# Other stage orders in a two-layer transformer kernel: constant stores on a second queue, two gate products ahead of the downs, and rearranged middle and attention stages

## The reference

```python
xn = _layernorm(x)
x = x + TTT(xn) + FFN(xn)          # layer 0
xn = _layernorm(x)
x = x + MLA(xn) + MoE(xn)          # layer 1
```

## Time and profile before

| | |
|---|---|
| median of 3 runs | 2130.93 us (2130.27 to 2133.2) |
| profiled execution | 2132.01 us |
| its span, first to last instruction | 2130.1 us |
| mean granted TensorE clock | 0.966 of full |
| TensorE busy | 1906.4 us, 89% |
| VectorE, ScalarE, GpSimd busy | 57%, 47%, 47% |
| DMA | 297.97 MB, mean 140 GB/s |

### The profile page before, as it was taken

The page is one execution under the profiler, slowest core; times in us unless marked ns, Lnnn a source line. Parts: engine busy times, 40 slices in busy tenths (PEclk is TensorE's granted clock), DMA queues, the critical chain, the costliest instruction groups (busy, mean ns, idle before and its releaser), DMA issues. The chain is left out here.

```text
span 2130.1 us, 34654 instructions
## 1 busy us (share of the span) xinstructions
PE 1906.4 (89%) x12632; PEld 1437.8 (67%) x12632; DVE 1208.6 (57%) x2367; ACT 1009.4 (47%) x2173; POOL 998.5 (47%) x765
## 2 busy tenths in 40 slices
PE   5897988899999999678999789999999999999997
PEld 3675767666666655567777567777777777777775
DVE  4662655686877764355243356555566555655552
ACT  3332646565565655466433235444444444444441
POOL 5443656455655544200233236555555555555551
PEclk9998999999999999789999889999999999999998
DMA  7875647336335432402677751222322223222211
GB/s 256 284 274 195 199 148 249 105 105 210 120 109 174 136 112 82 148 1 94 223 262 248 253 185 41 90 109 89 102 106 110 89 100 109 109 80 90 99 41 59
DMA packets 157111, 297.97 MB, mean 140 GB/s; under 512 B 20240, under 2 KB 97296, under 8 KB 150288
## 3 DMA queue, kind: packets, MB, share of 16 engines
q1 hardware_dynamic: 156944, 295.75, 41.2%
HBM read 221.52 MB, written 74.19 MB: 139 GB/s over the span
## 5 line engine op out<-in xcount | busy, mean ns | idle before, releaser
L1915 POOL TENSOR_SCALAR probs<-probs,rsum 128x512 f32<-128x512 f32 x256 | 397.5, 1569 | 362.1 <-DVE rsum L2047 362.1
L2011 ACT ACTIVATE p_tok<-bank 128x512 fp32r<-128x512 f32 x256 | 154.5, 606 | 403.4 <-PE bank L1955 403.3
L2043 DVE TENSOR_REDUCE nmax<-bank 128x1 f32<-128x512 f32 x256 | 158.9, 683 | 111.5 <-PE bank L1947 111.5
L2053 DVE TENSOR_TENSOR p_tok<-bank,p_tok 128x512 fp32r<-128x512 f32 x256 | 173.8, 681 | 22.6 <-ACT p_tok L2011 22.6
L2003 ACT ACTIVATE probs<-bank,nmax 128x512 f32<-128x512 f32 x256 | 172.2, 694 | 4.2 <-DVE nmax L2043 4.2
L60 PE MATMUL bank<-xs,ffn_w 128*128 128x512 f32 x352 | 153.4, 436 | 10.4 <-issue 8.4
L1955 PE MATMUL bank<-ident,probs 128*128 128x128 f32 x1024 | 156.6, 276 | 6.1 <-DVE p_tok L2053 5.9
L1423 POOL TENSOR_TENSOR y_pieces<-y_tok,y_pieces 128x512 fp32r<-128x512 f32 x48 | 61.6, 1298 | 208.4 <-ACT y_pieces L1635 208.4
L1955 PEld LDWEIGHTS bank<-ident,probs 128*128 128x128 f32 x1024 | 121.8, 141 | 55.3 <-issue 28.3
L1077 DVE SCALAR_TENSOR_TENSOR pt<-bank,t_mask 128x256 f32<-128x256 f32 x256 | 91.7, 414 | 101.1 <-PE bank L864 99.7
L61 PE MATMUL bank<-xs,ffn_w 128*128 128x512 f32 x352 | 138.9, 395 | 0.0
(11 more groups left out here) (271 smaller groups left out, 4906.9 us busy)
## 6 DMA issues: line engine op xcount, KB each, us to landing
ffn_w<-ffn_pieces SPq DMA_DIRECT2D x120, 512.0 KB, 3.6
uvo<-uvo_pieces SPq DMA_DIRECT2D x16, 2048.0 KB, 7.9
wq<-wq_pieces SPq DMA_DIRECT2D x16, 1536.0 KB, 6.4
ffn_pieces<-stage SPq DMA_DIRECT2D x30, 512.0 KB, 4.2
xs<-xn_pieces SPq DMA_DIRECT2D x4, 2048.0 KB, 8.4
y_tok<-in_gup SPq DMA_DIRECT2D x32, 256.0 KB, 3.1
wk<-wk_pieces SPq DMA_DIRECT2D x16, 512.0 KB, 3.6
ffn_w<-ffn_pieces SPq DMA_DIRECT2D x16, 384.0 KB, 3.5
```

The lines of the kernel that those rows point to most:

```text
L1915: nc.gpsimd.tensor_scalar(probs[:, u % 8, :], probs[:, u % 8, :], rsum[:, u % 8:u % 8 + 1], None, ALU.mult).then_inc(norm_done, 1)
L2011: nc.scalar.activation(p_tok[:, Q % 2, 0, :, hh * P:(hh + 1) * P], banks[4 + u % 2][:].rearrange("p (k q) -> p k q", k=NBLK), ACT.Copy).th ...
L2043: nc.vector.tensor_reduce(nmax[:, u % 8:u % 8 + 1], banks[u % HG][:], axis=X_AXIS, op=ALU.max, negate=True).then_inc(max_done, 1)
L2053: nc.vector.tensor_tensor(p_tok[:, Q % 2, 1, :, q], banks[4 + u % 2][:].rearrange("p (k q) -> p k q", k=NBLK), p_tok[:, Q % 2, 0, :, q].bi ...
```

## The change

Eight edits, all of order or of place; no product is added or left out.

1. Stage 1: the constants of the last tile are stored by ScalarE's queue instead of SyncE's, and SyncE issues `move_rates` behind the last tile's work instead of within it.
2. Stage 2's FFN order: two gate products instead of one stand ahead of each part's down products, and ahead of the first part. `wx` is cleared by VectorE, and GpSimd spreads the first keys ahead of its other two clearings.
3. Middle, first steps: the first four transpositions to tokens are issued at once; the bias products are made in four parts in steps -4 to -1; `ow_hi` is scaled by GpSimd, `ow_lo` is made in two halves; normalizing and splitting move by a step.
4. Middle, steps after: `high` and `low` of the older block come ahead of the newer block's normalizing and squaring.
5. Last expert: the eight pieces of the last group are placed as with the other experts (`fills`), and `TAIL` is reordered by one place.
6. Attention's first steps: four key projections in step -1, two in step 0, one each in steps 1 and 2. In the other groups the output products stand ahead of the projections of their slot, and the fourth step has its two query projections in slots 0 and 1 and the context in slot 2.
7. `rope_low` is done ahead of GpSimd's four scalings, and `rope_high` between the second and the third exponential.
8. End: the last group's output weights have a place of their own (`uvo_end`), the output products of the last two groups follow `CLOSING`, and three steps fewer follow at the end.

The diff, cut to these parts:

```diff
         def ffn_order():
-            order = [("gate", 0, 0)]
+            order = [("gate", 0, 0), ("gate", 0, 1)]
             for a, (lo, hi) in enumerate(THIRDS):
                 for i in range(lo, hi):
-                    order += [("gate", a, i)] if i > lo else []
+                    order += [("gate", a, i)] if i > lo + 1 else []
                     order += [("up", a, i)]
-                order += [("gate", a + 1, hi)] if a + 1 < len(THIRDS) else []
+                order += [("gate", a + 1, hi), ("gate", a + 1, hi + 1)] if a + 1 < len(THIRDS) else []
                 order += [("down", a, o) for o in range(NF)]
             return order
...
                                 load_x(t + 2)
-                            if slot == 0 and t == NTB - 1:
-                                move_rates()
-                        store_cst(t)
+                        if t < NTB - 1:
+                            store_cst(t)
+                    move_rates()
...
+                    for m in range(NF):
+                        q = NF * (NTB - 1) + m
+                        act.wait_ge(cst_done, q + 1)
+                        for e in range(2):
+                            act.dma_start(cst_dram[8 * m:8 * m + 8, NTB - 1, e, :, :],
+                                          cs[:, q % NCS, e * HX:(e + 1) * HX]).then_inc(cst_out[q % NCS], 16)
...
-                    nc.gpsimd.memset(wx[:], 0.0).then_inc(zero_done, 1)
+                    spread_k(0)
                     nc.gpsimd.memset(sg_bd[:], 0.0).then_inc(zero_done, 1)
                     nc.gpsimd.memset(grad_bd[:], 0.0).then_inc(zero_done, 1)
-                    spread_k(0)
                     spread_k(1)
...
+                    nc.vector.memset(wx[:], 0.0).then_inc(wx_zero, 1)
...
         uvo, tok = place("uvo", [P, 2, HG, HID], F32R, 24), place("ckv_tok", [P, 2, 2, NBLK, KVC], F32R, 40)
+        uvo_end = place("uvo_end", [P, 2, HG, HID], F32R, 64)
...
-        LAST = NBLK * (NG - 1) + 8
+        LAST = NBLK * (NG - 1) + 5
+
+        CLOSING = {NQD - 3: ((1, NG - 2, 0), (3, NG - 2, 1)), NQD - 2: ((2, NG - 2, 2),),
+                   NQD: ((0, NG - 2, 3), (1, NG - 1, 0), (2, NG - 1, 1)), NQD + 1: ((0, NG - 1, 2), (1, NG - 1, 3))}
 
         def att_jobs(n):
             p, G = (n + 1) % 4, (n + 1) // 4
             slots = [[], [], [], []]
+            if n < 3:
+                early = {-1: (0, 1, 2, 3), 0: (4, 5), 1: (6,), 2: (7,)}[n]
+                slots[0] += [("ctx", n - 1, 0)] if n >= 1 else []
+                for x, j in enumerate(early):
+                    slots[1 + x // 2].append(("proj", 1, j))
+                return slots
+            if p == 3 and G + 1 < NG:
+                return [[("proj", G + 1, 6)], [("proj", G + 1, 7)], [("ctx", n - 1, 0)], []]
             if 1 <= n <= NQD:
                 slots[0].append(("ctx", n - 1, 0))
+            if n >= 7 and p < 2 and (n - 7) // 4 < NG - 2:
+                slots[1].append(("out", (n - 7) // 4, 2 * p))
+                slots[3].append(("out", (n - 7) // 4, 2 * p + 1))
             if G + 1 < NG:
                 slots[1].append(("proj", G + 1, 2 * p))
                 slots[2].append(("proj", G + 1, 2 * p + 1))
-            if n >= 7 and p < 2 and (n - 7) // 4 < NG:
-                slots[1].append(("out", (n - 7) // 4, 2 * p))
-                slots[3].append(("out", (n - 7) // 4, 2 * p + 1))
...
             NJE = len(ejobs)
             FILL = {1: (0, 1), 2: (2, 3, 4), 3: (5, 6, 7)}
-            fills = lambda e, i: [NL + PER_G * e + x for x in (FILL.get(i, ()) if e + 1 < NEXP else range(PER_G) if i == NEI - 1 else ())]
-            TAIL = [("down", 0), ("down", 1), ("proj", 0), ("proj", 1), ("proj", 2), ("proj", 3), ("down", 2), ("proj", 4), ("down", 3),
-                    ("proj", 5), ("proj", 6), ("proj", 7)]
+            fills = lambda e, i: [NL + PER_G * e + x for x in (FILL.get(i, ()))]
+            TAIL = [("down", 0), ("down", 1), ("proj", 0), ("proj", 1), ("proj", 2), ("proj", 3), ("down", 2), ("proj", 4), ("proj", 5),
+                    ("down", 3), ("proj", 6), ("proj", 7)]
...
+                    pool.wait_ge(ow_in, 16)
+                    for k in range(NF):
+                        nc.gpsimd.tensor_scalar(ow_hi[:, k, :], ow_raw[:, k, :], small[:, SM["post_w"] + k:SM["post_w"] + k + 1], None, ALU.mult)\
+                            .then_inc(owhi_done, 1)
...
 
-                    def out_bias():
+                    def out_bias(o):
                         pe.wait_ge(ow_in, 16)
-                        for o in range(NF):
-                            for k in range(NF):
-                                ins = nc.tensor.matmul(banks[5][:, o:o + 1], ow_raw[:, k, o * P:(o + 1) * P], small[:, SM["post_b"] + k:SM["post_b"] + k + 1],
-                                                       start=(o + k == 0), stop=(k == NF - 1), skip_group_check=True)
-                        ins.then_inc(c_ready, 1)
+                        for k in range(NF):
+                            ins = nc.tensor.matmul(banks[5][:, o:o + 1], ow_raw[:, k, o * P:(o + 1) * P], small[:, SM["post_b"] + k:SM["post_b"] + k + 1],
+                                                   start=(o + k == 0), stop=(k == NF - 1), skip_group_check=True)
...
-                        if b is not None:
+                        for b in range(NBLK) if j == S0 else (j + 6,) if -3 < j <= NB - 7 else ():
                             to_tokens(0, b)
                         b = block_at(j, 4)
                         if b is not None:
...
-                            act.wait_ge(feat_ready[z], b - 1)
-                        nc.scalar.activation(y_tok[:, 2 * z + b % 2, :], tok_bank(z, b)[:], ACT.Square, bias=nsum[:, z, b:b + 1], scale=float(HID),
+                        if z == 1 and b >= 2:
+                            act.wait_ge(feat_ready[1], b - 1)
+                        square = y_tok[:, 2 + b % 2, :] if z == 1 else p_hi[:, 0, :]
+                        nc.scalar.activation(square, tok_bank(z, b)[:], ACT.Square, bias=nsum[:, z, b:b + 1], scale=float(HID),
...
                     def normalize(z, b):
                         act.wait_ge(nmr_done[z], b + 1)
+                        if z == 0 and b >= 2:
...
                     for j in range(S0, SE):
-                        b = block_at(j, 6)
-                        if b is not None:
-                            spread(0, b)
-                        b = block_at(j, 4)
-                        if b is not None:
-                            high(0, b)
-                        b = block_at(j, 6)
-                        if b is not None:
-                            normalize(0, b)
-                        if j == -2:
-                            act.wait_ge(ow_in, 16)
-                            act.wait_ge(cst_done, 2)
-                            for k in range(NF):
-                                nc.scalar.activation(ow_hi[:, k, :], ow_raw[:, k, :], ACT.Identity, bias=zero[:],
-                                                     scale=small[:, SM["post_w"] + k:SM["post_w"] + k + 1]).then_inc(owhi_done, 1)
+                        if j < -2:
+                            spread(0, j + 6)
+                            if j + 5 >= 0:
+                                normalize(0, j + 5)
+                            if j + 4 >= 0:
+                                high(0, j + 4)
+                        else:
+                            if j == -2:
+                                normalize(0, 3)
+                            b = block_at(j, 4)
+                            if b is not None:
+                                high(0, b)
+                            b = block_at(j, 5)
+                            if b is not None and j > -2:
+                                normalize(0, b)
+                            b = block_at(j, 6)
+                            if b is not None:
+                                spread(0, b)
                         if 0 <= j < NF:
...
                     nc.vector.memset(one[:], 1.0).then_inc(cst_done, 1)
+                    def ow_low(k):
+                        dve.wait_ge(owhi_done, k + 1)
+                        nc.vector.scalar_tensor_tensor(out=ow_lo[:, k, :], in0=ow_raw[:, k, :], scalar=small[:, SM["post_w"] + k:SM["post_w"] + k + 1],
+                                                       in1=ow_hi[:, k, :].bitcast(F32), op0=ALU.mult, op1=ALU.subtract).then_inc(owlo_done, 1)
+
+                    sums(0, 0)
                     for j in range(S0, SE):
-                        b = block_at(j, 6)
-                        if b is not None:
-                            sums(0, b)
-                            scales(0, b)
-                        b = block_at(j, 4)
-                        if b is not None:
-                            low(0, b)
-                        if j == -2:
-                            dve.wait_ge(c_ready, 1)
-                            nc.vector.tensor_copy(c_out[:], banks[5][:, 0:NF]).then_inc(c_done, 1)
```

(38 more changed lines are left out.)

45 lines of the change are left out of this document (31 added, 14 removed).

## The result

| | before | after |
|---|---|---|
| median | 2131.24 us (2130.27 to 2133.2) | 2067.56 us (2064.89 to 2069.34) |
| profiled execution | 2132.0 | 2065.9 |
| span of it | 2130.1 | 2064.0 |
| ratio | | 0.9699, 95% interval 0.9682 to 0.9716 |

A forecast was written before the change was run, and what follows sets the result against it. TensorE, busy 1906.4 of 2130.1 us, was taken as the bound. Savings of 7.5, 2, 9, 3, 14.5, 1, 33 and 10 summed to 80.0, from 2132.0 to 2052.0 us (median 2051), with 80 of 100 from 2032 to 2080.

The forecast's parts named there:

- Seam: Between stages 1 and 2: stage 2 starts at 191.6 instead of 199.2, saving 7.5 us (bounds 6.0 and 8.0).
- Two gates: Stage 2, ahead of the down products: a second gate product covers waits, saving 2 us (between -5.3 and +3).
- Start of the middle: Middle stage's start to its first output product: 9 us earlier (bounds -5 and -10.5).
- Normalizing: Middle stage's later steps: older block's high part first shortens waits for normalized pieces, saving 3 us (between -9 and +3).
- Start of attention: Attention's first steps: new key projection order saves 1 us (between -3 and +2); 0.8 for step 6 is counted here too.
- Even groups: Attention's even part: a group takes 51.46 us instead of 53.94, saving 33 us in all (bounds -41 and -14).
- Last expert: Last expert's pieces placed behind earlier up products: downs start earlier, saving 14.5 us (bounds -8 and -16).
- rival (c): Seam before attention fed late: loads hold query projections, 7 instead of 14.5, middle start gives 6; 2062 us, chance 0.11.
- End: End of attention: second place for the last weights removes the 8.0 wait, saving 10 us (between -6 and -13).
- Rival (a): Attention: ScalarE's order brings new waits near 1, a group saves only 1.0; 2075 us, chance 0.2.

## Why the prediction came out as it did

- Seam, 7.5 forecast, 4.0 in the mean: the step that failed is "SyncE ends with the rate loads near 187.7". It took their start (183.6) from the trace before, in which nothing was stored beside the rates; with the constants beside them they start at 186.4 to 189.2 and close the block. The 0.7 to 1.0 of barrier that it added is seen as 0.5 between the last landing and the first load. The Trainium skill (DMA: Bandwidth & Descriptors, Issuing engines are not separate DMA queues) says that DMAs of several issuing engines interleave on the same sixteen engines, and the traces agree: the rate stores take 3.58 us to land beside the constants and 1.41 without them. The saving at the seam is 4.6 to 5.4 us in the ten traces, under the 5.7 us of issuing, which the prediction gave as that rule's bound.
- Two gates, -2 forecast, +4.4 shown: the wrong sign, and beyond the +3 that was allowed. The step that failed is weighing the wait for hidden parts (5.3 us at most) against nothing but "some comes back". The scan's waits, 22.8 us, were the largest row of the same view and were not put into the sum.
- Start of the middle, right in size. The price of GpSimd and VectorE reading at once, which the prediction reckoned at 1.5 to 3 us by the Trainium skill's rule (SBUF — State Buffer, Who interferes with whom), is about 0.4: the first pair of weight differences takes 1.84 us beside GpSimd and 1.46 where ScalarE scales. GpSimd's scaling beside them takes 1.99 us instead of 1.56. By the rule one of the two stands still until the other is done; here the second difference takes 1.18 us and still ends before the scaling beside it does.
- Normalizing, 3 forecast: the order gives 0.9, the rest was never there. The prediction named the reason (the blocks are handed to and fro) and took a value above it. From the latents' wait to the last expert it takes 1.3 us more than before (171.8 against 170.5; 170.6 to 171.9 in the other traces). The clock is slow behind that wait, but not evenly: the first 12 products take 5.47 us here, 4.61 before, and 3.9 to 5.5 in the other traces, and where they are short the stretch is no shorter. The cause of the 1.3 stays open.
- Start of attention, -1.8 forecast, +1.0 measured: the sum named the mechanism (short steps, rope among the exponentials) and mis-sized it, at about 1.2 twice. The rope's place costs 4.1 in the one pair of traces and 2.9 in the other. Without it the stretch is 79.5 to 80.8, which is 1.8 to 3.1 less than before.
- Even groups: right by place and size, but the wait of 1.18 ahead of the scores was read as the rope's alone. The sum did not ask when the last query projection's low part is done. That the edit moves this projection forward as well, which made the forecast come true, was not reckoned with and is luck in that respect.
- Last expert: right by mechanism, place and size, and undone by itself. Its loads came in time, so rival (c) is not seen. End: right by place and size, as far as traces tell.
- Rival (a) has ScalarE's order hold things back with waits near 1: true of steps 2 and 4, and of the groups only when the order of jobs is undone.

## What to carry to other kernels

An engine's waits must be read as one balance: an edit that removes the second largest wait of a stage moves work between intervals, and the largest may grow by more. A wait that is priced from a trace holds only with the traffic of that trace beside it; when DMAs are moved to a second queue, what is in flight then can be slowed (here from 1.4 to 3.6 us) and become what closes the block. A view of waits names only one releaser, here the one that ended 0.25 us ahead of the other; before a wait is counted as saved, look up when everything else that the waiting instruction reads is ready. Edits to one engine's order can be a loss alone and a gain together, so a walk through all queues of a step, with each start, is worth more than a sum over the edits.

## What the runs showed of the hardware

TensorE's clock after one and the same row of waits differs between executions. The last context's 12 products come behind waits of 1.07, 1.23 and 1.50 us in both kernels. The windows (us, busy by engine, granted clock, DMA share, GB/s), of the changed kernel, whose mean clock of 0.62 comes from about half clock over most of the stretch and full clock at its end:

```profile
2042.10:2046.60 4.50, 4.44 (x13) 3.53 (x14) 0.00 (x0) 0.00 (x0) 0.00 (x0) 0.62 0.02 4
```

and of the one with the rope's place in the short steps:

```profile
2040.00:2043.00 3.00, 2.90 (x13) 2.42 (x14) 0.00 (x0) 0.00 (x0) 0.00 (x0) 1.00 0.00 0
```

The same 12 products take 4.58 us in the one and 3.00 in the other. Of the thirteen traces with the new end, these products take 4.4 to 4.6 us in ten and 3.0 in three, behind the same wait of 1.50; the stretch from step 59 on takes 80.2 to 80.6 us in the ten and 78.6 to 78.7 in the three. Such a place is worth about 1.6 us by chance, so differences of a few us between medians need the stretch in which they arise; why the clock fell in one and not in the other, the runs don't tell.
